# Conditioned FFN on one core: the beginning rebuilt (the q product, x's head sums, the order of the first loads)

## Chip, cores and metric

The kernel runs on one core of a Trainium2 chip. The metric is the device time of one execution in microseconds, the median of several runs; the profile is one further execution with the hardware profiler on.

## What is computed

x is 64 x 64 x 512 (batch, token, feature), cond is 64 x 256. Cut to what matters, the reference is:

```python
q_emb = relu(cond @ W3 + b3)                       # (64, 512)
x1 = (64 * x + x.sum(axis=1, keepdims=True)) * q_emb[:, None, :]
y = relu(x1 @ W2 + b2)                             # (64, 64, 512)
gates = top2(softmax(y @ W_router + b_router))     # six experts
out = x + y @ W_base + b_base + (y @ A_s) @ B_s + sum_e gates_e * (y @ A_r[e]) @ B_r[e]
```

## The kernel before

**Tiling.** The 4096 tokens are cut into 8 groups of 512 (eight batches of 64 tokens). The 512 features are four chunks of 128 partitions. For a group, m1 multiplies x1 with W2 (a bank of PSUM for each chunk of y), h gives router logits and the low-rank products, and m2 multiplies y with W_base into four tiles of 128 tokens. Each product of two f32 matrices is made of three matmuls: both operands are split into a rounded part "hi" (ScalarE copies it into the type fp32r) and a rest "lo" (VectorE or GpSimd subtract), and hi\*hi, lo\*hi and hi\*lo are added in PSUM.

**The first group** is prepared in another way than the rest. Its x comes in token order in four tiles of 128 tokens (L229) and TensorE transposes them, 16 transposes (L740), into four banks, one for each feature chunk. VectorE then works inside those banks: `sum_head` (L506 to L513) sums over the tokens of a batch and adds 64 x, `scale_head` (L515) multiplies by q, ScalarE makes x_hi out of the bank (`x1_split_head`, L375) and `rest_head` (L523) makes x_lo from the bank and x_hi. q itself is 16 matmuls with W3 as the weights, read with a stride of four columns, and cond (turned, 64 columns) as the moving side (`q`, L767); `q_relu` (L364) turns each of the four results into a chunk of qT. Dummy matmuls on a zero tile (`keep_warm`, L724) fill in.

**The later groups** are turned on VectorE (L474), summed (L479, L486), scaled by q on GpSimd (L308), split on ScalarE (`x1_split`, L344) and their rest is taken on VectorE out of SBUF (`x1_rest`, L491).

**What sets the order** is a hand-written program for each engine, with semaphores between them; there is no planner. On TensorE: dummies, the turns of cond, 16 turns of x, q's matmuls (L879 to L886), `m1_first` (L774 to L816), then h and m2 of group 0, then the other groups. On GpSimd: the rests of W2 in four pieces (L316 to L318), of the router and low-rank matrix Wd (L320), of W_base in four pieces (L321), then the scaling of group 1. SyncE issues the loads in the order x (4 tiles), W3 (2 halves), W2 (4), W_base and the small ones (L228 to L243). ScalarE issues cond, b2 and b3 (L336 to L338). cond and b2 are turned together and copied in one piece.

`m1_first` runs its 48 matmuls (4 chunks k of the features in, 4 tiles m out, 3 terms) in the order in which operands come to be, first k=0 and k=1 for all m, then k=2 and k=3 for the tiles 0 and 1, then for 2 and 3:

```python
for tiles in ((0, 1), (2, 3)):
    for k in range(KC // 2, KC):
        pe.wait_ge(x1_hi_ready, k + 1)
        pe.wait_ge(W2_lo_ready, k + 1)
        for m in tiles:
            chunk(m, k, W2_hi, x1_hi)
            chunk(m, k, W2_lo, x1_hi)
            pe.wait_ge(x1_lo_ready, k + 1)
            last = chunk(m, k, W2_hi, x1_lo)
```

Of the kernel before, what the change touches and what calls it, by code (L numbers as in the profile page):

```python
# [22 lines left out]
def adaln_ffn(nc, x, cond, W3, b3, W2, b2, W_base, b_base, A_s, B_s, A_r, B_r, W_router, b_router, out):  # L23
    F32 = mybir.dt.float32
# [24 lines left out]
    WARM_LOAD, WARM_W3, WARM_HALF, WARM_Q = 8, 1, 2, 1  # L49
# [7 lines left out]
    with ctx:  # L57
# [42 lines left out]
        vsum_head = sb("vsum_head", [P, KC, BG])  # L100
# [5 lines left out]
        cond_sb = sb("cond_sb", [B + KC, Q])  # L106
        condT = sb("condT", [P, KC + QC * B])
        qT = sb("qT", [P, KC, B])
        b3_sb = sb("b3_sb", [P, KC])
        b2_sb = condT[:, B:B + KC]  # L110
# [23 lines left out]
        m2_ps = [bank(f"m2_ps{t}") for t in range(TT)]  # L134
        m1_ps = [bank(f"m1_ps{m}") for m in range(KC - 1)] + [m2_ps[2]]
        hT = bank("hT")
        q_ps = m1_ps
        head_ps = [m2_ps[0], m2_ps[1], m2_ps[3], hT]
# [7 lines left out]
        cond_loaded, W3_loaded, b3_loaded = sem("cond_loaded"), [sem(f"W3_loaded{k}") for k in range(QC)], sem("b3_loaded")  # L146
        W2_loaded = [sem(f"W2_loaded{c}") for c in range(KC)]
# [66 lines left out]
        def _(sp):  # L214
# [12 lines left out]

            for t in range(TT):  # L228
                sp.dma_start(x_nat[0][:, t, :], x_groups[0][:, t, :]).then_inc(head_loaded[t], 16)  # L229
            for k in range(QC):  # L230
                sp.dma_start(W3_sb[:, k, :], W3[k * P:(k + 1) * P, :]).then_inc(W3_loaded[k], 16)
# [44 lines left out]
        def _(pool):  # L276
# [58 lines left out]
        def _(act):  # L335
            act.dma_start(cond_sb[0:B, :], cond).then_inc(cond_loaded, 16)  # L336
            act.dma_start(cond_sb[B:B + KC, 0:P], b2.rearrange("(k p) -> k p", p=P)).then_inc(cond_loaded, 16)
# [21 lines left out]
            nc.scalar.activation(condT[:, :], m1_ps[0][:, 0:KC + QC * B], ACT.Copy).then_inc(condT_copied, 1)  # L359
# [59 lines left out]
            def step(g, par):  # L419
# [8 lines left out]
                for m in range(KC):  # L428
                    relu(g, m, first)
                    if m == 0 and not first and not second:  # L430
                        hw_split(slice(0, TG), g)
# [35 lines left out]
        def _(dve):  # L467
# [255 lines left out]
        def _(pe):  # L723
# [13 lines left out]
            for t in range(TT):  # L737
                pe.wait_ge(head_loaded[t], 16)
                for c in range(KC):
                    turn = nc.tensor.transpose(head_ps[c][:, t * P:(t + 1) * P],  # L740
                                               x_nat[0][:, t, :].rearrange("p (f c) -> p c f", c=KC)[:, c], ident[:, :])
                    if t == TT - 1:
                        turn.then_inc(head_turned, 1)
# [212 lines left out]
```

## Time and profile before

| | |
|---|---|
| median of 3 runs | 236.16 us (236.14 to 236.66) |
| the profiled execution's own time | 236.26 us |
| its span, first to last instruction | 234.1 us |
| TensorE busy | 229.5 us, 98% of the span |
| VectorE, ScalarE, GpSimd busy | 165.8, 86.4 and 48.9 us |
| HBM read and written | 18.89 MB and 8.39 MB |

The own time is the span and 2.2 us around it. "PE" is TensorE's matmuls, "PEld" its weight loads, DVE is VectorE, ACT ScalarE, POOL GpSimd, SP SyncE. Busy matmul time counts the latency of each, so the pitch from one start to the next is what counts. PSUM tiles are grouped under one name: m_ps stands for the banks m1_ps and m2_ps.

### The profile page before, as it was taken

The numbers are of one execution on the slowest core, as the hardware profiler recorded it, in microseconds if no ns is written. First come the engines' busy times: TensorE is split into PE (matmuls) and PEld (weight loads), VectorE is DVE, ScalarE is ACT, GpSimd is POOL, SyncE is SP. The second block draws the span as 40 slices with busy tenths as digits, with TensorE's granted clock in tenths as the row PEclk, the third lists the DMA queues.
The fourth block names the chain that finished last, engine by engine and source line by source line (L and its number), as shares of the span: only waits on it lengthen the run. The fifth ranks groups of instructions, "written<-read, shape, count | busy, mean of one in ns | idle before, by whom it ended". The sixth has DMA issues, their size and how long they took to land.

```text
span 234.1 us, 3090 instructions
## 1 busy us (share of the span) xinstructions
PE 229.5 (98%) x1007; PEld 188.3 (80%) x1007; DVE 165.8 (71%) x309; ACT 86.4 (37%) x171; POOL 48.9 (21%) x57
## 2 busy tenths in 40 slices
PE   7999999999999999999999999999999999999994
PEld 3977888888888888888888888888888888888883
DVE  0685979899889966596939969399656966064344
ACT  3178632646036330535116240263306351252430
POOL 6089334032212211013012211022111030000000
PEclk9999999999999999999999999999999999999999
DMA  6999903509270723626053641709020360104004
GB/s 207 313 229 229 276 5 79 137 3 315 67 187 4 250 111 69 144 107 255 10 134 69 194 167 26 185 4 345 12 34 0 141 218 14 21 0 179 3 0 179
DMA packets 32505, 28.80 MB, mean 123 GB/s; under 512 B 5817, under 2 KB 22909, under 8 KB 32494
## 3 DMA queue, kind: packets, MB, share of 16 engines
q1 hardware_dynamic: 30682, 28.50, 43.1%
q10 hardware_dynamic: 1812, 0.17, 0.6%
q8 instruction: 6, 0.10, 0.2%
q14 instruction: 5, 0.04, 0.0%
HBM read 18.89 MB, written 8.39 MB: 117 GB/s over the span
## 4 chain that ended last, share of the span: by engine, by line
PE 97%; DVE 1%; ACT 1%; issue 0%; DVEq 0%
PE m_ps L750 78%; PE hT L750 9%; PE m_ps L777 5%; PE m_ps L727 2%; DVE out_nat L628 1%; PE m_ps L740 1%; PE m_ps L769 1%; PE hT L740 0%; ACT qT L367 0%; ACT W_hi L373 0%; ACT x_hi L378 0%; PE m_ps L734 0%; DVE idle L468 0%; PE hT L877 0%; PE m_ps L733 0%
## 5 line engine op out<-in xcount | busy, mean ns | idle before, releaser
L308 POOL TENSOR_TENSOR x_full<-x_sum,qT 128x512 f32<-128x512 f32 x28 | 32.2, 1150 | 134.6 <-DVE x_sum L486 134.6
L353 ACT ACTIVATE y_hi<-m_ps,condT 128x512 fp32r<-128x512 f32 x32 | 22.0, 687 | 77.5 <-PE m_ps L750 77.2
L750 PE MATMUL m_ps<-Wb_lo,y_hi 128*128 128x512 f32 x128 | 49.8, 389 | 0.0
L750 PE MATMUL m_ps<-Wb_hi,y_lo 128*128 128x512 f32 x128 | 49.8, 389 | 0.0
L750 PE MATMUL m_ps<-Wb_hi,y_hi 128*128 128x512 f32 x128 | 49.8, 389 | 0.0
L750 PE MATMUL m_ps<-x_hi,W_hi 128*128 128x512 f32 x112 | 43.6, 389 | 0.0
L750 PE MATMUL m_ps<-x_hi,W_lo 128*128 128x512 f32 x112 | 43.6, 389 | 0.0
L500 DVE TENSOR_TENSOR y_lo<-m_ps,y_hi 128x512 fp32r<-128x512 f32 x32 | 21.6, 674 | 30.4 <-ACT m_ps L355 30.4
L750 PE MATMUL m_ps<-x_lo,W_hi 128*128 128x512 f32 x112 | 41.8, 389 | 0.0
L474 DVE STREAM_TRANSPOSE xT<-x_quart 128x512 f32<-128x512 f32 x28 | 30.3, 1083 | 0.0
L750 PEld LDWEIGHTS m_ps<-Wb_hi,y_hi 128*128 128x128 f32 x128 | 24.0, 188 | 5.0
L750 PEld LDWEIGHTS m_ps<-Wb_hi,y_lo 128*128 128x128 f32 x128 | 24.0, 188 | 5.0
L750 PEld LDWEIGHTS m_ps<-Wb_lo,y_hi 128*128 128x128 f32 x128 | 24.0, 188 | 5.0
L347 ACT ACTIVATE x_hi<-x_full 128x512 fp32r<-128x512 f32 x28 | 17.6, 629 | 19.1 <-POOL x_full L308 19.0
L750 PEld LDWEIGHTS m_ps<-x_hi,W_hi 128*128 128x128 f32 x112 | 21.0, 188 | 4.4
L750 PEld LDWEIGHTS m_ps<-x_hi,W_lo 128*128 128x128 f32 x112 | 21.0, 188 | 4.4
L750 PEld LDWEIGHTS m_ps<-x_lo,W_hi 128*128 128x128 f32 x112 | 21.0, 188 | 4.3
L628 DVE TENSOR_TENSOR out_nat<-m_ps,x_nat 128x512 f32<-128x512 f32 x32 | 20.5, 680 | 2.1 <-PE m_ps L750 2.1
L355 ACT ACTIVATE m_ps<-m_ps,condT 128x512 f32<-128x512 f32 x32 | 21.0, 655 | 0.0
L486 DVE SCALAR_TENSOR_TENSOR x_sum<-xT,vsum 128x512 f32<-128x512 f32 x28 | 19.4, 693 | 2.1
L494 DVE TENSOR_TENSOR x_lo<-x_full,x_hi 128x512 fp32r<-128x512 f32 x28 | 19.1, 706 | 1.6 <-ACT x_hi L347 1.6
L479 DVE TENSOR_REDUCE vsum<-xT 128x8 f32<-128x512 f32 x28 | 19.0, 679 | 0.3
(99 smaller groups left out, 256.5 us busy)
## 6 DMA issues: line engine op xcount, KB each, us to landing
out_dram<-out_nat SPq DMA_DIRECT2D x32, 256.0 KB, 2.2
x_quart<-in_x_dram SPq DMA_DIRECT2D x28, 256.0 KB, 4.5
x_nat<-in_x_dram SPq DMA_DIRECT2D x7, 1024.0 KB, 6.1
gatesT<-wT SPq DMA_DIRECT2D x28, 48.0 KB
x_nat<-in_x_dram SPq DMA_DIRECT2D x4, 256.0 KB, 3.7
W_f<-in_L_cond_W_dram SPq DMA_DIRECT2D x4, 256.0 KB, 6.7
Wb_f<-in_L_ffn_W_base_dram SPq DMA_DIRECT2D x1, 1024.0 KB, 9.2
W_sb<-in_L_cond_W_dram SPq DMA_DIRECT2D x2, 256.0 KB, 5.0
```

Source lines behind the costliest of these rows:

```text
L308: nc.gpsimd.tensor_tensor(per_batch(x1_full[:, c, :]), per_batch(x1_sum[:, c, :]), qT[:, c, bass.ds(BG * g, BG)].unsqueeze(2).to_broadcast ...
L347: nc.scalar.activation(x1_hi[par][:, c, :], x1_full[:, c, :], ACT.Copy).then_inc(x1_hi_ready, 1)
L353: nc.scalar.activation(y_hi[:, m, :], m1_ps[m][:, :], ACT.Relu, bias=b2_sb[:, m:m + 1]).then_inc(y_hi_ready, 1)
L355: nc.scalar.activation(m1_ps[m][:, :], m1_ps[m][:, :], ACT.Relu, bias=b2_sb[:, m:m + 1]).then_inc(y_full_ready, 1)
L474: nc.vector.transpose(xT[c % 2][:, :], x_quart[par][:, :, :].rearrange("p b (i c) -> p c b i", c=KC)[:, c]).then_inc(xT_ready, 1)
L479: nc.vector.tensor_reduce(vsum[c % 2][:, :], per_batch(xT[c % 2][:, :]), AX.X, ALU.add).then_inc(vsum_ready, 1)
L486: nc.vector.scalar_tensor_tensor(out=per_batch(x1_sum[:, c, :]), in0=per_batch(xT[c % 2][:, :]), scalar=float(N), in1=vsum[c % 2][:, :].un ...
L494: nc.vector.tensor_tensor(x1_lo[par][:, c, :], x1_full[:, c, :], x1_hi[par][:, c, :].bitcast(F32), ALU.subtract).then_inc(x1_lo_ready, 1)
L500: nc.vector.tensor_tensor(y_lo[:, m, :], m1_ps[m][:, :], y_hi[:, m, :].bitcast(F32), ALU.subtract).then_inc(y_lo_ready, 1)
L628: nc.vector.tensor_tensor(out_nat[par][:, t, :], m2_ps[t][:, :], x_nat[par][:, t, :], ALU.add).then_inc(out_ready, 1)
L750: mm = nc.tensor.matmul(psum, lhsT, rhs, start=start and i == 0, stop=stop and i == len(terms) - 1)
L777: return nc.tensor.matmul(m1_ps[m][:, :], W[:, k, m * P:(m + 1) * P], x1[0][:, k, :], start=k == 0 and W is W2_hi and x1 is x1_hi, stop=k ...
```

## The change

Only the beginning is touched; the loop over the groups is the same.

- **q.** Only q's first chunk is still made directly (W3 strided as weights, two matmuls). The other three come from `q_others`: cond as weights (64 columns), W3 streamed contiguously, 256 columns for each matmul, four of them. The result lies with batches on the partitions; ScalarE copies it in two pieces to SBUF, TensorE turns it back in three transposes, then the three `q_relu`. These transposes stand inside `m1_first`.
- **x's sums by token halves.** The banks of the head hold two feature chunks for 256 tokens each, so that the first half can be summed when two tiles of x are there. The products with q go out of PSUM into SBUF: chunk 0 once into x1_hi directly and once into x1_full, the others into x1_full. ScalarE splits chunks 1 to 3 from there with `x1_split`, and the rests are taken with `x1_rest` out of SBUF, chunk 1's on GpSimd.
- **Loads.** W3's first (upper) half is issued ahead of the last tile of x.
- **The rest.** b2 is turned by itself after the first tile of x. Two single dummies stand behind the second and third tile of x, in place of one and two and one around q. `m1_first` takes the tiles in the order 0, 3, 2 and then 1. In the second half both x_hi terms of a pair of tiles go ahead of the wait for x_lo. The last piece of Wb_hi is made after the first relu. Group 1's first sum moves behind one more `y_rest`.

```diff
-    WARM_LOAD, WARM_W3, WARM_HALF, WARM_Q = 8, 1, 2, 1
+    WARM_LOAD, WARM_X = 8, 1
...
+        head_ps = [ctx.enter_context(nc.psum_tensor(f"head_ps{i}", [P, 2, 512], F32)) for i in range(2)]
+        q_rows = x1_sum[0:B, 0, 0:(KC - 1) * P]
...
             for t in range(TT):
+                if t == TT - 1:
+                    load_W3(0)
                 sp.dma_start(x_nat[0][:, t, :], x_groups[0][:, t, :]).then_inc(head_loaded[t], 16)
+            load_W3(1)
...
                 W_rest(W2_lo[:, c, :], W2_f[:, c, :], W2_hi[:, c, :], W2_lo_ready)
+                if c == 1:
+                    pool.wait_ge(x1_hi_ready, 2)
+                    pool.wait_ge(x1_lo_ready, 1)
+                    W_rest(x1_lo[0][:, 1, :], x1_full[:, 1, :], x1_hi[0][:, 1, :], x1_lo_ready)
...
             q_relu(0)
-            q_relu(1)
             W2_split(0)
-            q_relu(2)
-            x1_split_head(0)
-            q_relu(3)
-            x1_split_head(1)
+            for half in range(2):
+                act.wait_ge(q_rows_done, half + 1)
+                feats = slice(half * (P // 2), (half + 1) * (P // 2))
+                nc.scalar.activation(q_rows.rearrange("b (c f) -> b c f", f=P)[:, :, feats],
+                                     m1_ps[1 + half][0:B, 0:D // 2].rearrange("b (f c) -> b c f", c=KC)[:, 1:KC],
+                                     ACT.Copy).then_inc(q_rows_copied, 1)
             W2_split(1)
+            for c in range(1, KC):
+                q_relu(c)
+            x1_split(0, 0, 1)
             W2_split(2)
-            x1_split_head(2)
             W2_split(3)
+            x1_split(0, 0, 2)
+            x1_split(0, 0, 3)
...
+            sum_head(0, 0)
+            add_head(0, 0, 1)
+            sum_head(0, 1)
+            sum_head(1, 0)
+            add_head(1, 0, 3)
+            dve.wait_ge(qT_ready, 1)
+            dve.wait_ge(x1_sum_ready, 2)
+            nc.vector.tensor_tensor(by_half(x1_hi[0][:, 0, :]), head_chunk(0), q_spread(0),
+                                    ALU.mult).then_inc(x1_hi_ready, 1)
+            full_head(0)
+            dve.wait_ge(x1_full_ready, 1)
+            x1_rest(0, 0, 0)
+            full_head(1)
+            add_head(0, 1, 2)
+            sum_head(1, 1)
+            add_head(1, 1, 4)
+            full_head(2)
+            full_head(3)
+            dve.wait_ge(x1_lo_ready, 2)
+            x1_rest(0, 0, 2)
+            x1_rest(0, 0, 3)
...
+            turn_head(0)
+            pe.wait_ge(condT_copied, 1)
+            pe.wait_ge(b2_loaded, 16)
+            nc.tensor.transpose(m1_ps[0][:, QC * B:QC * B + KC], b2_rows[:, :], ident[0:KC, 0:KC]).then_inc(b2_turned, 1)
+            for t in range(1, TT - 1):
+                turn_head(t)
+                keep_warm(WARM_X)
...
+            def q_others(k, half):
+                cols = slice(half * (D // 2), (half + 1) * (D // 2))
+                mm = nc.tensor.matmul(m1_ps[1 + half][0:B, 0:D // 2], condT[:, cond_cols(k)], W3_sb[:, k, cols],
+                                      start=(k == 0), stop=(k == QC - 1))
...
                 pe.wait_ge(W2_hi_ready, 1)
-                for m in range(KC - 1):
-                    pe.wait_ge(qT_ready, m + 1)
-                    chunk(m, 0, W2_hi, x1_hi)
+                chunk(0, 0, W2_hi, x1_hi)
+                chunk(3, 0, W2_hi, x1_hi)
+                pe.wait_ge(q_rows_copied, 2)
+                chunk(2, 0, W2_hi, x1_hi)
+                for c in range(1, KC):
+                    last = nc.tensor.transpose(m1_ps[1][:, (c - 1) * B:c * B], q_rows[:, (c - 1) * P:c * P],
+                                               ident[0:B, 0:B])
+                last.then_inc(q_done, 1)
...
                         for m in tiles:
                             chunk(m, k, W2_hi, x1_hi)
                             chunk(m, k, W2_lo, x1_hi)
-                            pe.wait_ge(x1_lo_ready, k + 1)
+                        pe.wait_ge(x1_lo_ready, k + 1)
+                        for m in tiles:
                             last = chunk(m, k, W2_hi, x1_lo)
...
+            pe.wait_ge(b2_copied, 1)
+            q_first(0)
+            q_others(0, 0)
+            turn_head(TT - 1)
+            q_others(0, 1)
+            q_first(1)
+            for half in range(2):
+                q_others(1, half)
```

## Rows read from the trace of the kernel before

**Rows 1.** The page: TensorE's granted clock in 40 slices, in tenths.

```profile
PEclk9999999999999999999999999999999999999999
```

**Rows 2.** Chain that ended last, the beginning: start us, us, what.

```profile
12.47 11.47 PE m_ps L777 x48
...
28.70 22.44 PE m_ps L750 x99
```

**Rows 3.** Timeline, TensorE: start us, us, engine line op out<-in xcount [idle before].

```profile
1.27 3.59 PE L727 MATMUL m_ps<-idle 128*128 128x512 bf16 x8 [1.27 <-DVE idle L468]
...
4.97 0.37 PE L734 MATMUL m_ps<-ident,cond_sb 64*128 64x64 f32 x1
...
6.19 0.84 PE L740 MATMUL m_ps<-ident,x_nat 128*128 128x128 f32 x3
...
7.04 0.56 PE L740 MATMUL m_ps<-ident,x_nat 128*128 128x128 f32 x3
...
7.56 0.52 PE L740 MATMUL m_ps<-ident,x_nat 128*128 128x128 f32 x3
...
8.04 0.38 PE L727 MATMUL m_ps<-idle 128*128 128x512 bf16 x1
8.25 1.40 PE L769 MATMUL m_ps<-condT,W_sb 128*128 128x64 f32 x6
9.49 0.59 PE L727 MATMUL m_ps<-idle 128*128 128x512 bf16 x2
9.92 1.40 PE L769 MATMUL m_ps<-condT,W_sb 128*128 128x64 f32 x6
...
23.78 0.39 PE L750 MATMUL hT<-y_hi,Wd_hi 128*128 128x512 f32 x1
```

**Rows 4.** Timeline, VectorE, the head of group 0.

```profile
7.88 0.69 DVE L507 TENSOR_REDUCE vsum_head<-m_ps 128x8 f32<-128x512 f32 x1 [6.67 <-PE m_ps L740]
8.60 0.70 DVE L510 SCALAR_TENSOR_TENSOR m_ps<-m_ps,vsum_head 128x512 f32<-128x512 f32 x1
9.21 0.68 DVE L507 TENSOR_REDUCE vsum_head<-m_ps 128x8 f32<-128x512 f32 x1
...
13.77 0.70 DVE L510 SCALAR_TENSOR_TENSOR m_ps<-m_ps,vsum_head 128x512 f32<-128x512 f32 x1
14.58 0.70 DVE L519 TENSOR_TENSOR m_ps<-m_ps,qT 128x512 f32<-128x512 f32 x1
...
17.91 0.68 DVE L526 TENSOR_TENSOR x_lo<-m_ps,x_hi 128x512 fp32r<-128x512 f32 x1
```

**Rows 5.** Timeline, ScalarE, the same stretch.

```profile
10.49 0.72 ACT L367 ACTIVATE qT<-m_ps,b_sb 128x64 f32<-128x64 f32 x2 [4.84 <-PE m_ps L769]
11.11 0.62 ACT L373 ACTIVATE W_hi<-W_f 128x512 fp32r<-128x512 f32 x1
...
15.31 0.60 ACT L378 ACTIVATE x_hi<-m_ps 128x512 fp32r<-128x512 f32 x1 [1.12 <-DVE m_ps L519]
```

**Rows 6.** Timeline, GpSimd, the rests of the weights.

```profile
11.81 1.27 POOL L314 TENSOR_TENSOR W_lo<-W_f,W_hi 128x512 fp32r<-128x512 f32 x1 [7.02 <-ACT W_hi L373]
13.75 2.54 POOL L314 TENSOR_TENSOR W_lo<-W_f,W_hi 128x512 fp32r<-128x512 f32 x2 [0.67 <-ACT W_hi L373]
...
17.75 1.30 POOL L314 TENSOR_TENSOR Wd_lo<-Wd_f,Wd_hi 128x512 fp32r<-128x512 f32 x1
```

**Rows 7.** All instructions of L308 and of L494: duration ns min/median/max, starts.

```profile
L308 POOL TENSOR_TENSOR x_full<-x_sum,qT x28: 1043/1046/1422, 25.7 to 191.3; 128x512 f32<-128x512 f32 x28
...
L494 DVE TENSOR_TENSOR x_lo<-x_full,x_hi x28: 649/682/1531, 38.6 to 196.4; 128x512 fp32r<-128x512 f32 x28
```

**Rows 8.** Timelines of VectorE and of GpSimd where these two extremes lie.

```profile
39.20 1.53 DVE L494 TENSOR_TENSOR x_lo<-x_full,x_hi 128x512 fp32r<-128x512 f32 x1
...
38.76 1.42 POOL L308 TENSOR_TENSOR x_full<-x_sum,qT 128x512 f32<-128x512 f32 x1 [1.41 <-DVE x_sum L486]
```

**Rows 9.** Time to landing of W3's halves (issued at 2.67 and 3.14).

```profile
DMA to landing us min/median/max: 4.8/5.0/5.1
```

More of the change, by code:

```diff
@@ L128, in adaln_ffn @@
         pick_one = sb("pick_one", [S, P])
-        m2_ps = [bank(f"m2_ps{t}") for t in range(TT)]
+        head_ps = [ctx.enter_context(nc.psum_tensor(f"head_ps{i}", [P, 2, 512], F32)) for i in range(2)]
+        m2_ps = [head_ps[0][:, 0, :], head_ps[0][:, 1, :], bank("m2_ps2"), head_ps[1][:, 0, :]]
         m1_ps = [bank(f"m1_ps{m}") for m in range(KC - 1)] + [m2_ps[2]]
-        hT = bank("hT")
-        q_ps = m1_ps
-        head_ps = [m2_ps[0], m2_ps[1], m2_ps[3], hT]
+        hT = head_ps[1][:, 1, :]
         x_loaded = [sem(f"x_loaded{i}") for i in range(2)]
@@ L429, in step @@
                     relu(g, m, first)
+                    if first and m == 0:
+                        Wb_split(KC - 1)
                     if m == 0 and not first and not second:
@@ L510, in sum_head, with add_head @@
+            def add_head(h, pr, summed):
+                dve.wait_ge(vsum_head_ready, summed)
                 nc.vector.scalar_tensor_tensor(
[L511 to L512 removed]
+                    out=head_half(pr, h), in0=head_half(pr, h), scalar=float(N),
+                    in1=vsum_head[:, h, pr, :].unsqueeze(2).to_broadcast([P, BG, N]),
@@ L731, in _, with turn_head @@
             pe.wait_ge(ident_ready, 1)
-            pe.wait_ge(cond_loaded, 32)
-            nc.tensor.transpose(m1_ps[0][:, 0:B + KC], cond_sb[:, 0:P], ident[0:B + KC, 0:B + KC])
-            last = nc.tensor.transpose(m1_ps[0][:, cond_cols(1)], cond_sb[0:B, P:2 * P], ident[0:B, 0:B])
+            pe.wait_ge(cond_loaded, 16)
+            for k in range(QC):
+                last = nc.tensor.transpose(m1_ps[0][:, cond_cols(k)], cond_sb[:, k * P:(k + 1) * P], ident[0:B, 0:B])
             last.then_inc(condT_done, 1)
-            for t in range(TT):
+            def turn_head(t):
                 pe.wait_ge(head_loaded[t], 16)
                 for c in range(KC):
-                    turn = nc.tensor.transpose(head_ps[c][:, t * P:(t + 1) * P],
+                    begin = (c % 2) * (TG // 2) + (t % 2) * P
+                    turn = nc.tensor.transpose(head_ps[c // 2][:, t // 2, begin:begin + P],
                                                x_nat[0][:, t, :].rearrange("p (f c) -> p c f", c=KC)[:, c], ident[:, :])
-                    if t == TT - 1:
+                    if t % 2 == 1 and c % 2 == 1:
                         turn.then_inc(head_turned, 1)
-            keep_warm(WARM_W3)
+            turn_head(0)
[5 more added lines that the diff above has]
+                keep_warm(WARM_X)
             def product(psum, terms, start, stop):
@@ L782, in m1_first @@
                 pe.wait_ge(W2_hi_ready, 1)
-                for m in range(KC - 1):
-                    pe.wait_ge(qT_ready, m + 1)
-                    chunk(m, 0, W2_hi, x1_hi)
+                chunk(0, 0, W2_hi, x1_hi)
[6 more added lines that the diff above has]
+                last.then_inc(q_done, 1)
                 pe.wait_ge(W2_lo_ready, 1)
-                for m in range(KC - 1):
+                for m in (0, 2, 3):
                     chunk(m, 0, W2_lo, x1_hi)
+                pe.wait_ge(x1_lo_ready, 1)
+                for m in (0, 2, 3):
+                    chunk(m, 0, W2_hi, x1_lo)
                 pe.wait_ge(qT_ready, KC)
-                chunk(KC - 1, 0, W2_hi, x1_hi)
-                chunk(KC - 1, 0, W2_lo, x1_hi)
-                pe.wait_ge(x1_lo_ready, 1)
-                for m in range(KC):
-                    chunk(m, 0, W2_hi, x1_lo)
+                chunk(1, 0, W2_hi, x1_hi)
+                chunk(1, 0, W2_lo, x1_hi)
+                chunk(1, 0, W2_hi, x1_lo)
                 for k in range(1, KC // 2):
```

101 lines of the change are left out of this document (44 added, 57 removed).

## The prediction

> **What bounds the kernel now.** I read the chain that ended last first. Behind 12.47 us it is TensorE alone: 48 matmuls of `m1_first` in 11.47 us, then 99 in 22.44, a pitch of 0.227 us [rows 2]. Nothing after the beginning waits, so the change can move only two things: when `m1_first` starts, and how much it loses inside. Its own work is 48 x 0.227 = 10.88 us; h begins at 23.78 [rows 3], 11.31 after the start, so 0.43 is lost inside. **The mark to beat is 23.78.** Then the timelines of the first 24 us: TensorE turns x until 8.04 and does q until past 11.2 [rows 3]; VectorE begins at 7.88, when the last tile is turned [rows 4]; ScalarE waits 4.84 us for q and makes qT at 10.49 [rows 5]. The start is a meeting of q and x's sums.
>
> **The clock.** The granted clock reads full in all slices [rows 1], but eight dummies of 512 columns take 3.59 us, 0.43 apiece as at 1.2 GHz; four transposes take 0.85 from 6.19 and 0.48 from 7.56 [rows 3]. The level of 2.4 GHz comes at about 7.1. Up to 6.2 the new order issues the same work, so I keep 7.1.
>
> **The change, part by part.**
>
> *Up to W3.* The last tile's four transposes leave this place (-0.48), b2's own turn comes in (one more small transpose, at most 0.37 [rows 3]; I take 0.3), and there is one dummy more (0.21). The first W3 matmul stays at 8.25 [rows 3]. Chunk 1 of tile 1 is then turned near 6.9 and VectorE starts its first half sum at about 7.2, not 7.88.
>
> *The loads.* W3's first half lands 4.8 us after its issue at 2.67, at 7.5 [rows 9], and is used at 8.25: nobody waits. A place earlier it gains nothing, and the last x tile, then at about 7.5, is wanted at 8.9. This part is worth 0; its cover is 0.7 us on either side.
>
> *q.* 16 matmuls of 64 columns cost 0.21 each (six in 1.24) and three dummies go. In come two of those and four `q_others` of 256 columns with an f32 moving side, which no row shows. Lower bound: the 512-column pitch by columns, 0.11. Upper: the 64-column one times four, 0.83. They are far apart; I take the middle, 0.48, as a weight load of the old form costs something that does not grow with columns. TensorE: 8.25 first chunk, 8.45 `q_others`, 8.93 to 9.41 the last x tile (its chunk 1 at 9.05), 9.41 `q_others`, 9.89 the first chunk's second half, then two `q_others` to 11.06.
> The Trainium skill (FP8 and Floating Point Precision, TensorE Precision Notes) says that true FP32 takes four passes; 256 columns at 2.4 GHz would be 0.43, and no run here shows it yet. By it every time below would be some 0.1 earlier.
>
> *The start.* x: 9.05 + 0.32 (from the transpose at 7.56 to the sum at 7.88) = 9.37 for the second half's sum, +0.72 the addition [rows 4], +0.81 the product (13.77 to 14.58) = 10.90. q: 9.89 + 0.57 (9.92 to 10.49) + 0.35 = 10.81. VectorE is the later by a hair. The product goes straight to x1_hi; the next engine follows 0.73 later (14.58 to 15.31 [rows 4, 5]): **`m1_first` starts at 11.63, 0.84 earlier.** W2_hi is there at 11.4.
>
> *Inside.* ScalarE copies q's rows by 12.0 (W2_split 0.62 between, two copies of some 0.3). TensorE does chunks 0 and 3, then 2, then three transposes: 0.5 that the old order did not have, and back to work at 12.9. qT's second chunk: 12.7 + 0.35 ScalarE + 0.35 = VectorE's product of chunk 1 at s = 13.40. Nine more matmuls for k=0 end at 14.95, k=1 at 17.67. x1_hi of chunk 1: s + 0.73 + 0.63 = 14.76, in time. VectorE's next steps are two of 0.61, one of 0.72, one of 0.81, so chunk 2's product is at s + 2.75 and its x1_hi at s + 4.14 = 17.54, in time by 0.13.
>
> *The new wait.* Before, `rest_head` read the bank and one SBUF tile, and ran 0.68 beside GpSimd (17.91, inside 17.75 to 19.05 [rows 4, 6]). `x1_rest` reads two SBUF tiles. That form has a median of 682 ns and a maximum of 1531 [rows 7], and that maximum stands against GpSimd's maximum: VectorE's at 39.20 ends at 40.73, 0.55 after GpSimd's at 40.18, which itself took 1.42 for 1.05 because the rest before it held on until 39.28 [rows 7, 8]. They take turns, whole instructions at a time. In the head GpSimd has no pause: chunk 1's rest from s + 1.44, then pieces of W2_lo at a pitch of 1.25 (two in 2.54 [rows 6]), the last from s + 3.94 to s + 5.23 = 18.63. VectorE asks for chunk 2's rest at s + 4.14, 0.2 too late: done at 18.63 + 0.55 = 19.18; TensorE wanted it at 17.67 + 4 x 0.227 = 18.58. Then Wd_lo, queued behind W2_lo, has its turn (1.29 less 0.14 for what it did while it waited, as 1.05 became 0.90 above) to 20.33, and chunk 3's rest ends at 20.88. TensorE wanted it at 19.18 + 6 x 0.227 = 20.54. 14 matmuls remain: end at 20.88 + 3.17 = **24.05, against 23.78: +0.27.**
> The Trainium skill says the same (SBUF — State Buffer, Who interferes with whom): a VectorE instruction with two SBUF inputs contends with a GpSimd instruction that reads SBUF, by an exclusive lock held for the whole instruction, and issue order decides who blocks. By this rule, the trace agrees (1531 ns). It speaks against this change; without it the sum would be 0.6 faster than before.
>
> *Behind it.* y's splits follow the last products by ScalarE; Wb_hi's last piece inside costs relu 1 a step of 0.6, and GpSimd reaches Wb_lo's first piece at some 22, before m2 asks at 25. The regrouping of terms makes m1_done of tile 0 two matmuls later, 0.45, hidden by h starting only 3 us on. I cost these at 0; if that cover is gone, y_lo's last chunk is late next, by 0.1 to 0.3.
>
> **Sum.** 236.26 (own time) + 0.27 = 236.5; the own time lies 0.10 above the median, so **236.4 us.** With the start's bounds: at 0.11 a `q_others` s falls only to 13.1, as VectorE and ScalarE bind: 236.1; at 0.83, see below.
>
> **Rivals.**
> A, the forecast: start won, given back by the shared turns. 0.42.
> B, VectorE gets the first turn. Its request is only 0.2 behind GpSimd's start, and these are sums of five steps. Then chunk 2's rest is in time, W2_lo's last piece ends at 19.38 for 19.03, and m1 ends at 23.46: -0.32, 235.8. For it: the small gap. Against: every step from s on has its own row and s cancels. 0.18.
> C, no stall: TensorE runs through from 12.9, m1 ends at 17.67 + 24 x 0.227 = 23.11, -0.67, 235.5; with cheap `q_others` down to 235.3. For it: 27 of 28 rests of this form are near 0.68 [rows 7]. Against: only in the head is GpSimd busy without pause. 0.25.
> D, the other side: streaming W3 in f32 costs in proportion, 0.83. Then q's first chunk is at 10.59, the start at 12.2 and s at 14.4, one us later, with m1's end at 25.05: +1.27, 237.4. It decides from about 0.6 a matmul: above that q, not x, is the last to arrive, three `q_others` weigh on s, and the time is over 236.9. For it: nothing in the trace has an f32 moving side of this width. 0.13.
> E, the beginning only shifts its waits and nothing changes, 236.2. 0.02.
>
> **How the numbers follow.** A measurement of this kernel tells some 0.3%, 0.71 us, from no change: faster is below 235.45, slower above 236.87. A gives same 0.33, slower 0.09 (q's price above the middle); B same 0.15, faster 0.03; C faster 0.17, same 0.08; D slower 0.13; E same 0.02. In all faster 0.20, same 0.58, slower 0.22. Range 235.3 to 237.1: it takes in A to C with the bounds of q's price, and leaves most of D and C's edge out. A's own range is 236.1 to 236.9.
>
> **What would show it.** In the new profile: `m1_first`'s first matmul at 11.4 to 11.8; `q_others` at a pitch near 0.5; the turns of b2 and the three transposes 0.2 to 0.5 us of TensorE each; a rest (L494's successor) of over 1 us against W2_lo's last piece, and another against Wd_lo; TensorE waiting 0.6 and 0.3 us for them; h's first matmul near 24.05 and from there the old pitch. Wrong if the rests take 0.68 beside GpSimd (then C), if TensorE waits ahead of 12 us for x1_hi longer than before (D), if the 2.4 GHz level comes after 8 us, or if anything behind 24 us waits.

## The result and the profile after

The changed kernel takes 236.50 us (median of 22 runs, 236.09 to 238.54), the one before 236.03 (22 runs, 235.23 to 236.66), run in turns on the same chips. The ratio is 1.0039, with a 95% interval of 1.0024 to 1.0053: slower by some 0.4%. The profiled execution took 236.53 us against 236.26, its span is 234.8 us against 234.1. The forecast was 236.4, with 235.3 to 237.1 as its range; 18 of the 22 runs lie between 236.09 and 236.92, four at 238.3 to 238.5.

The timeline of TensorE in the changed kernel, from the first matmul with W3 to h (a line stands for consecutive instructions of one form; several lines between are left out):

```profile
7.60 0.47 PE L820 MATMUL m_ps<-condT,W_sb 128*128 128x64 f32 x2
8.00 0.65 PE L828 MATMUL m_ps<-W_sb,condT 128*64 128x256 f32 x2
8.57 0.75 PE L784 MATMUL head_ps<-ident,x_nat 128*128 128x128 f32 x4
9.25 0.65 PE L828 MATMUL m_ps<-W_sb,condT 128*64 128x256 f32 x2
9.83 0.68 PE L820 MATMUL m_ps<-condT,W_sb 128*128 128x64 f32 x2
10.44 1.08 PE L828 MATMUL m_ps<-W_sb,condT 128*64 128x256 f32 x4
11.64 0.97 PE L836 MATMUL m_ps<-x_hi,W_hi 128*128 128x512 f32 x3
12.53 0.40 PE L847 MATMUL m_ps<-ident,x_sum 64*128 64x64 f32 x3
...
18.44 0.39 PE L836 MATMUL m_ps<-x_hi,W_lo 128*128 128x512 f32 x1
19.16 0.74 PE L836 MATMUL m_ps<-x_lo,W_hi 128*128 128x512 f32 x2 [0.34 <-DVE x_lo L527]
...
20.43 0.39 PE L836 MATMUL m_ps<-x_hi,W_lo 128*128 128x512 f32 x1
20.87 0.73 PE L836 MATMUL m_ps<-x_lo,W_hi 128*128 128x512 f32 x2
...
24.18 0.39 PE L800 MATMUL head_ps<-y_hi,Wd_hi 128*128 128x512 f32 x1
```

`m1_first` begins at 11.64, 0.83 us earlier than before, but h at 24.18, 0.40 later than the 23.78 of [rows 3]: from start to h it is 12.54 us against 11.31. Two steps between matmuls stand out against the pitch of 0.227: 0.73 to 19.16 and 0.44 to 20.87. Behind each the next step is again long (two matmuls end 0.74 and 0.73 after the start of the first, where 0.61 is usual). What they waited for stands in VectorE's and GpSimd's timelines, the answer to [rows 7, 8]:

```profile
12.21 1.08 DVE L527 TENSOR_TENSOR x_lo<-x_full,x_hi 128x512 fp32r<-128x512 f32 x1
...
17.50 1.61 DVE L527 TENSOR_TENSOR x_lo<-x_full,x_hi 128x512 fp32r<-128x512 f32 x1 [0.17 <-ACT x_hi L372]
19.03 1.78 DVE L527 TENSOR_TENSOR x_lo<-x_full,x_hi 128x512 fp32r<-128x512 f32 x1
...
16.02 2.54 POOL L335 TENSOR_TENSOR W_lo<-W_f,W_hi 128x512 fp32r<-128x512 f32 x2
18.60 1.67 POOL L335 TENSOR_TENSOR Wd_lo<-Wd_f,Wd_hi 128x512 fp32r<-128x512 f32 x1
20.22 3.00 POOL L335 TENSOR_TENSOR Wb_lo<-Wb_f,Wb_hi 128x512 fp32r<-128x512 f32 x2
```

Read the ends: GpSimd's W2_lo ends at 18.56, VectorE's rest at 19.11; GpSimd's Wd_lo at 20.27, VectorE's second rest at 20.81. Each time 0.55 us of work follow the other's end, and Wd_lo itself became 1.67 us long where it takes 1.30 [rows 6], because it had to let the rest end first. Chunk 0's rest at 12.21 was held too: it took 1.08 us and ended 0.54 after GpSimd's first piece of W2_lo (12.75). That one cost nothing that shows: the next product waits for qT's second chunk, which is ready at the same moment, 13.29.

Behind h a second loss shows, near 55 us, in group 1. TensorE's last matmul starts at 231.15 against 230.52, 0.63 later. Of that 0.40 are from the head and 0.23 come behind h, 0.18 of them in the two long steps here (0.31 to 55.31 and 0.34 to 55.65; before, 0.23 and 0.24):

```profile
55.00 0.39 PE L800 MATMUL head_ps<-y_hi,Wd_lo 128*128 128x512 f32 x1
55.31 0.50 PE L800 MATMUL head_ps<-y_lo,Wd_hi 128*128 128x512 f32 x1
55.65 0.40 PE L800 MATMUL head_ps<-Wb_hi,y_hi 128*128 128x512 f32 x1
```

VectorE is late with y_lo. Its chain goes back without a pause of note to the routing of group 0, where one subtraction on 24 columns, read from two SBUF tiles, met GpSimd's Wu_lo:

```profile
31.24 1.00 DVE L592 TENSOR_TENSOR logit<-h_nat,lmax 128x24 f32<-128x24 f32 x1
...
30.90 1.30 POOL L335 TENSOR_TENSOR Wu_lo<-Wu_f,Wu_hi 128x512 fp32r<-128x512 f32 x1
```

Before, it met it as well, but took 0.66 us:

```profile
30.84 0.66 DVE L551 TENSOR_TENSOR logit<-h_nat,lmax 128x24 f32<-128x24 f32 x1
...
30.16 1.29 POOL L314 TENSOR_TENSOR Wu_lo<-Wu_f,Wu_hi 128x512 fp32r<-128x512 f32 x1
```

GpSimd's Wu_lo now comes 0.74 us later (30.90 against 30.16) and VectorE's step only 0.40, so it stands longer.

### The profile page after: what moved, and what is told of

It is laid out like the page before. It is cut to its first block, busy times and chain, and to the rows that moved or that the text cites. A ratio compares the mean times of both kernels' runs of the same rounds, so it can differ in the third digit from the quotient of the medians.

```text
span 234.8 us, 3094 instructions
## 1 busy us (share of the span) xinstructions
PE 229.7 (98%) x1005; PEld 186.1 (79%) x1005; DVE 168.4 (72%) x309; ACT 86.9 (37%) x173; POOL 51.4 (22%) x58
## 4 chain that ended last, share of the span: by engine, by line
PE 93%; DVE 4%; ACT 1%; issue 0%; DVEq 0%
PE m_ps L800 44%; PE head_ps L800 44%; PE m_ps L836 2%; PE m_ps L769 2%; DVE x_lo L527 1%; DVE out_nat L669 1%; PE head_ps L784 1%; DVE x_full L558 1%; DVE head_ps L545 1%; PE m_ps L828 0%; PE m_ps L820 0%; DVE x_hi L568 0%; ACT qT L396 0%; ACT x_hi L372 0%; DVE vsum_head L540 0%
## 5 line engine op out<-in xcount | busy, mean ns | idle before, releaser
L378 ACT ACTIVATE y_hi<-m_ps,b_sb 128x512 fp32r<-128x512 f32 x32 | 22.1, 689 | 78.0 <-PE m_ps L800 76.6
L800 PE MATMUL head_ps<-Wb_hi,y_hi 128*128 128x512 f32 x96 | 37.4, 389 | 0.0
L800 PE MATMUL head_ps<-Wb_hi,y_lo 128*128 128x512 f32 x96 | 37.4, 389 | 0.0
L800 PE MATMUL head_ps<-Wb_lo,y_hi 128*128 128x512 f32 x96 | 37.3, 389 | 0.0
L527 DVE TENSOR_TENSOR x_lo<-x_full,x_hi 128x512 fp32r<-128x512 f32 x31 | 23.6, 783 | 1.8 <-ACT x_hi L372 1.8
L380 ACT ACTIVATE m_ps<-m_ps,b_sb 128x512 f32<-128x512 f32 x32 | 21.0, 658 | 0.0
L800 PEld LDWEIGHTS head_ps<-Wb_hi,y_lo 128*128 128x128 f32 x96 | 18.0, 188 | 3.8
L800 PEld LDWEIGHTS head_ps<-Wb_lo,y_hi 128*128 128x128 f32 x96 | 18.0, 188 | 3.7
L800 PEld LDWEIGHTS head_ps<-Wb_hi,y_hi 128*128 128x128 f32 x96 | 18.0, 188 | 3.7
L478 ACT ACTIVATE h_head<-head_ps,h_bias 32x128 f32<-32x128 f32 x32 | 11.5, 360 | 12.8 <-PE head_ps L800 12.2
```

Source lines behind the costliest of these rows:

```text
L378: nc.scalar.activation(y_hi[:, m, :], m1_ps[m][:, :], ACT.Relu, bias=b2_sb[:, m:m + 1]).then_inc(y_hi_ready, 1)
L380: nc.scalar.activation(m1_ps[m][:, :], m1_ps[m][:, :], ACT.Relu, bias=b2_sb[:, m:m + 1]).then_inc(y_full_ready, 1)
L478: nc.scalar.activation(h_head[q * S:(q + 1) * S, :], hT[0:S, q * P:(q + 1) * P], ACT.Identity, bias=h_bias[0:S, 0:1]).then_inc(h_head_read ...
L527: nc.vector.tensor_tensor(x1_lo[par][:, c, :], x1_full[:, c, :], x1_hi[par][:, c, :].bitcast(F32), ALU.subtract).then_inc(x1_lo_ready, 1)
L800: mm = nc.tensor.matmul(psum, lhsT, rhs, start=start and i == 0, stop=stop and i == len(terms) - 1)
```

## The experiments

Each ran in turns with the kernel before, whose median was 235.72 to 235.93 us in those turns. So the ratio in the last column compares two rows better than their medians do. The high level of TensorE's clock comes at another time in each profiled execution (last section), which moves the start by more than 2 us. The stretch from `m1_first`'s first matmul to h's does not follow it: e1, e5, e10 and e11 have 11.56 to 11.58 us with starts from 11.16 to 13.80, the changed kernel, e4 and e6 12.54 with starts from 11.64 to 12.02.

| kernel | start, h, between (us) | median, runs | ratio to before, 95% |
|---|---|---|---|
| before | 12.47, 23.78, 11.31 | 236.03, 22 | 1 |
| changed | 11.64, 24.18, 12.54 | 236.50, 22 | 1.0024 to 1.0053 |
| e1 rests from PSUM | 13.47, 25.05, 11.58 | 235.64, 12 | 0.9982 to 1.0000 |
| e2 GpSimd holds back | 12.06, 24.26, 12.20 | 236.25, 11 | 1.0012 to 1.0046 |
| e3 old, rests from SBUF | 12.70, 25.51, 12.81 | 237.37, 4 | 1.0045 to 1.0074 |
| e4 Wu's rest earlier | 11.92, 24.46, 12.54 | 236.38, 12 | 1.0008 to 1.0053 |
| e5 is e1 and e4 | 11.16, 22.73, 11.57 | 235.33, 12 | 0.9969 to 1.0003 |
| e6 load order back | 12.02, 24.56, 12.54 | 237.69, 6 | 1.0062 to 1.0113 |
| e7 q all direct | 11.98, 24.58, 12.60 | 236.78, 10 | 1.0023 to 1.0063 |
| e8 is e7, e1 and e4 | 12.07, 24.42, 12.35 | 236.77, 12 | 1.0013 to 1.0063 |
| e9 is e8 with dummies | 12.32, 23.71, 11.39 | 235.48, 12 | 0.9988 to 1.0005 |
| e10 is e5, chunk 0 sooner | 11.41, 22.97, 11.56 | 235.23, 12 | 0.9970 to 1.0016 |
| e11 is e10, more dummies | 13.80, 25.36, 11.56 | 235.49, 13 | 0.9971 to 0.9996 |

### e1: the rests read from PSUM

```diff
-                nc.vector.tensor_tensor(by_half(x1_full[:, c, :]), head_chunk(c), q_spread(c),
+                out = x1_full[:, c, :] if c < 2 else head_ps[0][:, c - 2, :]
+                nc.vector.tensor_tensor(by_half(out), head_chunk(c), q_spread(c),
...
-            x1_rest(0, 0, 2)
-            x1_rest(0, 0, 3)
+            for c in (2, 3):
+                dve.wait_ge(x1_hi_ready, c + 1)
+                nc.vector.tensor_tensor(x1_lo[0][:, c, :], head_ps[0][:, c - 2, :],
+                                        x1_hi[0][:, c, :].bitcast(F32), ALU.subtract).then_inc(x1_lo_ready, 1)
```

(ScalarE's two splits read the same banks.)

> The changed kernel, but the products of chunks 2 and 3 go into the two PSUM banks that chunks 0 and 1 have left, and ScalarE and VectorE read them there, so that a rest has one SBUF input. Theory (VectorE and GpSimd take turns for the second SBUF input): both rests fall from 1.61 and 1.78 us to about 0.68, TensorE's two waits at 18.4 and 20.4 us go, h's first matmul comes at 23.2 to 23.4 instead of 24.18, and the time is 0.8 to 0.9 us lower, 235.6. Rival (the rests are late because x1_hi of chunk 2 is late, whoever holds a port): the rests may get shorter, but TensorE still waits 0.3 us or more at each, h comes at 23.8 or later and the time is within 0.4 us of 236.5.

Measured: 235.64 us, 0.86 below the changed kernel (1.1 by the ratios). Both rests run beside GpSimd, which is never idle there (VectorE's timeline, then GpSimd's):

```profile
19.31 1.29 DVE L584 TENSOR_TENSOR x_lo<-head_ps,x_hi 128x512 fp32r<-128x512 f32 x2
...
17.84 2.54 POOL L335 TENSOR_TENSOR W_lo<-W_f,W_hi 128x512 fp32r<-128x512 f32 x2
20.40 1.29 POOL L335 TENSOR_TENSOR Wd_lo<-Wd_f,Wd_hi 128x512 fp32r<-128x512 f32 x1
```

Two rests in 1.29 us, and from start to h it is 11.58, so 0.96 less. h came at 25.05 and not at 23.3, since in this execution (237.37 us) the clock's high level came more than 4 us later; the stretch and the median carry the verdict. The rival falls: x1_hi comes at the same distance from the start (the first of the two rests begins 5.84 us behind it here, 5.86 in the changed kernel), and TensorE has no step above 0.25 us between 16 and 56 us.

### e2: GpSimd holds back

```diff
             pool.wait_ge(Wd_hi_ready, 1)
+            pool.wait_ge(x1_lo_ready, KC)
```

> The changed kernel, but GpSimd waits for all four rests before Wd_lo. Theory (turns): the first rest stays at 1.6 us (W2_lo's last piece holds it), the second falls from 1.78 to about 0.7, so TensorE's second wait, 0.2 us and a slow restart, goes; h at 23.85 instead of 24.18, time lower by 0.3 us, 236.2. Wd_lo and Wb_lo end a good 0.6 us later, which nobody should feel. Rival (the second rest is long for another reason, for example that it waits for ScalarE): it stays at 1.7 us, and nothing changes, 236.5.

```profile
17.93 1.61 DVE L528 TENSOR_TENSOR x_lo<-x_full,x_hi 128x512 fp32r<-128x512 f32 x1 [0.17 <-ACT x_hi L373]
...
19.46 0.68 DVE L528 TENSOR_TENSOR x_lo<-x_full,x_hi 128x512 fp32r<-128x512 f32 x1
```

The first rest, held by W2_lo's last piece, stays at 1.61 us; the second falls from 1.78 to 0.68 as nothing else was changed than what GpSimd does at that moment. The stretch loses 0.34 us. The median is 0.25 lower, but the two intervals overlap, so here the trace carries the verdict; h came at 24.26 and not at 23.85, since the start was 0.42 later. So each of the two turns has its own share: 0.34 for Wd_lo's, the rest of e1's 0.96 for that of W2_lo.

### e3: the same rests in the old kernel

```diff
-                nc.vector.tensor_tensor(per_batch(head_ps[c][:, :]), per_batch(head_ps[c][:, :]),
+                nc.vector.tensor_tensor(per_batch(x1_full[:, c, :]), per_batch(head_ps[c][:, :]),
```

(and the splits and rests read x1_full.)

> The kernel before, with one thing of the change alone: the head's products go to SBUF and the splits and rests are read from there. Theory (turns): GpSimd makes W2_lo, Wd_lo and Wb_lo from 11.8 us on nearly without pause, so the four rests become 1.1 to 1.8 us each against 0.68, VectorE's head falls behind by 2 us or more, TensorE waits, and h comes 0.8 to 1.6 us later than 23.78: 236.9 to 237.7. Rival (reading from SBUF costs nothing, as this form has a median of 682 ns): h at 23.8, time within 0.2 us of 236.1.

```profile
15.88 1.19 DVE L526 TENSOR_TENSOR x_lo<-x_full,x_hi 128x512 fp32r<-128x512 f32 x1
...
19.12 1.78 DVE L526 TENSOR_TENSOR x_lo<-x_full,x_hi 128x512 fp32r<-128x512 f32 x2
...
20.35 0.50 PE L777 MATMUL m_ps<-x_lo,W_hi 128*128 128x512 f32 x1 [1.47 <-DVE x_lo L526]
```

This one part of the change alone makes the old kernel 0.6% slower (237.37 us), with one wait of 1.47 us and 1.50 us more from start to h. Three of the four rests took 1.16 to 1.19 us and the last 0.68, less than I expected for each. How long one takes depends on how far GpSimd is in its own instruction when the rest is asked for: the three end 0.55 us after GpSimd's (13.84, 17.07 and 20.30 against 13.29, 16.52 and 19.75), and the last falls into a pause of GpSimd's. VectorE is later each time, and the delays add up.

### e4: Wu's rest ahead of one scaling

```diff
             scale(1, 0)
-            scale(1, 1)
             pool.wait_ge(Wu_hi_ready, 1)
             W_rest(Wu_lo[:, :], Wu_f[:, :], Wu_hi[:, :], Wu_lo_ready)
+            scale(1, 1)
```

> The changed kernel, but GpSimd makes the rest of Wu before the scaling of group 1's second chunk, not after. Theory for the 0.2 us that TensorE loses near 55 us: the small subtraction of the logits at 31.24 us took 1.00 us (0.66 before) because it has two SBUF inputs and GpSimd was in Wu_lo; VectorE's chain stays 0.7 us behind and y_lo comes late. Then here the subtraction takes 0.2 to 0.3 us, the wait near 55 us goes, h's first matmul stays at 24.18 and the time is lower by 0.2 us, 236.3. Rival (that wait comes from the shift by 0.4 us of the whole start): it stays, and the time is 236.5.

```profile
31.52 0.18 DVE L592 TENSOR_TENSOR logit<-h_nat,lmax 128x24 f32<-128x24 f32 x1
...
55.31 0.40 PE L800 MATMUL head_ps<-y_hi,Wd_lo 128*128 128x512 f32 x1
55.55 0.40 PE L800 MATMUL head_ps<-y_lo,Wd_hi 128*128 128x512 f32 x1
55.78 0.39 PE L800 MATMUL head_ps<-Wb_hi,y_hi 128*128 128x512 f32 x1
```

The subtraction takes 0.18 us (1.00), with GpSimd idle beside it, and the two long steps near 55 us are gone (0.24 and 0.23), though the stretch to h is still 12.54. In the trace the cause of these two steps is settled. In the medians it is 0.12 us, less than these runs can tell.

### e5: both cures

> Both cures together: the rests of chunks 2 and 3 read from PSUM, and Wu's rest made before the scaling of group 1's second chunk. Theory: the two losses lie in different places (19 to 21 us and 55 us), so they add: 0.9 and 0.2 us less than the changed kernel, 235.4; no pause of TensorE over 0.3 us between 12 us and the end except the restarts in the first three microseconds of m1_first. Rival (a third wait takes the place): a new pause of VectorE's or ScalarE's making appears behind 24 us and the time is that of the first cure alone, 235.6 to 235.7, or more.

235.33 us, 1.17 below the changed kernel (1.25 by the ratios), where 0.9 and 0.2 were expected. Behind 13 us no step between TensorE's matmuls exceeds 0.25 us. No third wait took their place.

### e6: the old order of the loads

```diff
-                if t == TT - 1:
-                    load_W3(0)
                 sp.dma_start(x_nat[0][:, t, :], x_groups[0][:, t, :]).then_inc(head_loaded[t], 16)
+            load_W3(0)
             load_W3(1)
```

> The changed kernel with SyncE's loads in the old order: W3's first half behind the last tile of x. Theory: nobody waits for either in the new order (W3's half landed at 7.16 and is used at 7.6, the last x tile landed at 7.90 and is used at 8.57), and in the old order W3's half would land near 7.5 to 7.9: no change, 236.4 to 236.6. Rival (the order is what lets q start early): the first W3 matmul slips by 0.2 to 0.5 us, the last to arrive is q, so m1_first and the time slip by as much, 236.7 to 237.0.

```profile
7.06 0.38 PE L768 MATMUL m_ps<-idle 128*128 128x512 bf16 x1
7.80 0.65 PE L819 MATMUL m_ps<-condT,W_sb 128*128 128x64 f32 x2 [0.36 <-DMA W_sb<-in_L_cond_W_dram]
```

My theory fell, the rival held in its direction: TensorE waits 0.36 us for W3, the start is at 12.02, and the time is higher (237.69 in 6 runs that spread from 236.86 to 238.61; the profiled one, 236.86, is the fastest, 0.33 above that of the changed kernel, and its start 0.38). The stretch from start to h is the same, 12.54. By the ratios the old order costs 1.2 us; the trace explains 0.4 of it, and the rest stays open: the slower runs were not profiled.

### e7, e8 and e9: q direct, and what the clock makes of it

```diff
-            q_first(0)
-            q_others(0, 0)
-            turn_head(TT - 1)
-            q_others(0, 1)
-            q_first(1)
-            for half in range(2):
-                q_others(1, half)
+            for c in range(KC):
+                q_direct(0, c)
+            turn_head(TT - 1)
+            for c in range(KC):
+                q_direct(1, c)
```

(`q_direct` is the old `q`; the copies of rows and the three transposes go, and TensorE waits behind the first matmul of `m1_first` for all four chunks of qT.)

> The changed kernel with q made as before (W3 as strided weights, 64 columns of cond, for all four chunks), the rest of the change as it is; no copies of rows and no three transposes. Theory: a direct matmul costs 0.47 us (two records at 0.233), a streamed one 0.58, so q's first chunk is finished 0.3 us later behind four directs than behind one direct and one streamed, m1_first starts at about 11.9 to 12.0, q's last chunk is ready near 12.7, and what the transposes cost (0.65 us) is saved but waited for; the two rests still lose their turns, so h comes within 0.3 us of 24.2 to 24.5 and the time is 236.5 to 236.8. Rival (the transposes inside m1_first are a real loss): h at 23.6 or earlier and 235.9.

> q all direct, with both cures (rests from PSUM, Wu's rest earlier). Theory: without the turns the end of m1_first is set by TensorE's own work and by when x1_hi comes; q direct starts 0.3 us later and saves transposes it then waits for, so 235.4 to 235.8, no better than the streamed form with both cures. Rival (streaming W3 is a loss once the turns are cured): 235.1 or lower.

e7 took 236.78 us, e8 236.77. For e7 that is the number expected; e8 missed by 1 us. Both have something that neither theory knew. TensorE in three stretches of e7 (us, busy and count, granted clock, DMA share, GB/s):

```profile
10.00:12.00 2.00, 1.72 (x9) 0.99 1.11 375
12.50:15.20 2.70, 2.70 (x8) 0.50 1.18 209
15.50:20.00 4.50, 4.50 (x21) 1.00 1.06 222
```

The first two of them in e8:

```profile
10.00:12.00 2.00, 1.84 (x8) 0.87 1.12 366
12.50:15.20 2.70, 2.70 (x8) 0.56 1.10 198
```

With q all direct the granted clock falls to its lower level, 1.2 GHz, around the start of `m1_first`, and stays there for some 3 us: 8 matmuls in 2.7 us, 0.427 apart. In the changed kernel and the one before it is 1.00 in this stretch.

Every run lists its mean granted clock, and this tells the price of the fall. In e8 three runs of 12 have 1.000 and took 235.38 to 235.58 us, which is what my theory said; the other nine have 0.991 to 0.993 and took 236.54 us or more. In e7 nine runs of 10 have 0.985 to 0.993, and the one with 1.000 took 236.64, in their midst. So in e8 the fall costs some 1.3 us (median of the nine against the three), and in e7 nothing that shows. There the two rests still run against GpSimd (1.59 and 1.78 us), yet TensorE has no step above 0.25 us between 16 and 56 us: slowed by the clock, it comes when they are done. So the fall likely takes the place of the waits and does not add to them. e7's number was right with a fall in it that the theory did not have.

e9 is e8 with the old kernel's dummies around q:

```diff
-            for c in range(KC):
-                q_direct(0, c)
+            for c in range(KC - 1):
+                q_direct(0, c)
+            keep_warm(2)
             turn_head(TT - 1)
```

(one more dummy behind the second half, the fourth chunk last.)

> The kernel of e8 (q all direct, rests from PSUM, Wu's rest earlier) with the three dummy matmuls of the old kernel put back around q: two behind the first half of the first three chunks, one behind the second half, the fourth chunk last. In e8 the granted clock fell to 0.56 between 12.5 and 15.2 us and TensorE's pitch was 0.427 us there. Theory (64-column matmuls alone leave TensorE too lightly used, and the dummies or the 256-column streams keep the clock up): the granted clock stays at 1.00 from 10 to 20 us, no pitch of 0.427 behind 12 us, the start is 0.2 to 0.4 us later than e8's 12.07, and the time falls from 236.8 to 235.6 to 236.0. Rival (the fall has to do with the pause ahead of m1_first, or with chance): the clock falls as in e8 and the time is 236.8 or more.

The same two stretches in e9:

```profile
10.00:12.00 2.00, 2.00 (x12) 1.00 1.09 377
12.50:15.20 2.70, 2.58 (x12) 1.00 1.23 247
```

The clock stays at 1.00, the time falls by 1.29 us to 235.48 (1.0 by the ratios), and the 12 runs lie within 0.41 us. All 12 have a mean granted clock of 1.000, against 3 of 12 in e8 and 1 of 10 in e7, so it is not chance. In e7 and e8 TensorE had done eight direct matmuls and four transposes between 7.4 and 11.8 us, then paused 0.2 to 0.3 us for x1_hi; in e9 it had three dummies among them and no such pause before 12.3. The pause is not what lets the clock fall in e8, as it falls while the last direct matmul is still running, which ends at 11.84 (in e7 it falls at 11.97, at the end of the pause):

```profile
11.40:11.50 0.10, 0.10 (x2) 0.92 1.13 385
11.50:11.60 0.10, 0.10 (x2) 0.50 1.20 424
```

So the dummies hold the clock by what TensorE does ahead of the pause. Which of the three is needed, no run here shows.

### e10 and e11

```diff
             turn_head(TT - 1)
-            q_others(0, 1)
             q_first(1)
+            q_others(0, 1)
```

> The kernel of e5 with q's first chunk finished ahead of the second streamed matmul and not behind it. In the changed kernel VectorE had been ready for 0.35 us when qT's first chunk came, so q, not x, sets the start. Theory: q_relu comes 0.5 us earlier, the additions of x then set the start, so m1_first starts 0.3 us earlier than at e5's 11.16 (at the same clock), but the rows' copies and the three transposes come no earlier, so that at most 0.1 to 0.3 us of it is kept: 235.1 to 235.3 against 235.33. Rival (W3's second half is not there yet, it landed between 8.15 and 8.66): TensorE waits and nothing is gained, 235.3 to 235.6.

235.23 us against 235.33, within what these runs can tell; the start did not come earlier in the profiled one (11.41, with W3's first matmul 0.36 later; from that matmul to the start it is 3.98 us against 4.09). Not shown either way.

```diff
-    WARM_LOAD, WARM_X = 8, 1
+    WARM_LOAD, WARM_X = 8, 2
```

> The kernel of e10 with two dummies instead of one behind the second and the third tile of x (0.43 us more of TensorE before W3 at the high clock). In e5 and e10 four of 24 runs lay 1.6 to 2.3 us above the rest, in the kernel with direct q and dummies none of 12. Theory (the fuller use of TensorE in the first 9 us brings the high level in time in every run): the start moves from 11.4 to 11.5 to 11.8, the median rises by 0.1 to 0.4 us, to 235.3 to 235.6, and no run lies more than 1 us above the lowest. Rival (when the level comes is up to chance, whatever TensorE does): one to three of the dozen runs still lie 1.5 us or more above the lowest.

The rival held: one of 13 runs, the profiled one, took 237.47 us, the others 234.99 to 235.89. (One of 13 against four of 24 doesn't tell whether such runs became rarer.) Its transposes and dummies kept the long pitch (0.213 and 0.427 us) until about 10 us:

```profile
7.38 1.06 PE L773 MATMUL m_ps<-idle 128*128 128x512 bf16 x2
8.23 1.06 PE L788 MATMUL head_ps<-ident,x_nat 128*128 128x128 f32 x4
9.08 1.06 PE L773 MATMUL m_ps<-idle 128*128 128x512 bf16 x2
9.94 0.52 PE L824 MATMUL m_ps<-condT,W_sb 128*128 128x64 f32 x2
```

e1's did the same, with one dummy in each place:

```profile
7.38 0.63 PE L773 MATMUL m_ps<-idle 128*128 128x512 bf16 x1
7.81 1.06 PE L788 MATMUL head_ps<-ident,x_nat 128*128 128x128 f32 x4
8.66 0.63 PE L773 MATMUL m_ps<-idle 128*128 128x512 bf16 x1
9.09 0.53 PE L824 MATMUL m_ps<-condT,W_sb 128*128 128x64 f32 x2
```

(Here a dummy takes 0.43 us from start to start; the changed kernel's two between 6 and 8 us took 0.22.)

## Why the prediction was right, point by point

**The new wait** was the step that carried the forecast, and it stands to a tenth: s = 13.31 (13.40 forecast), the first rest done at 19.11 (19.18), the second at 20.81 (20.88), TensorE's waits 0.50 and 0.22 us (0.60 and 0.34). e1 and e2 show the cause by taking it away from VectorE's side and from GpSimd's; e3 puts it into the old kernel. The rule of the Trainium skill (SBUF — State Buffer, Who interferes with whom), that a VectorE instruction with two SBUF inputs contends with a GpSimd instruction that reads SBUF, agrees with all three (0.68 to 0.69 us a rest in e1, 0.68 for the freed one in e2, 1.16 to 1.19 for three of e3's). In [rows 7] only one of 28 rests had shown it. That chunk 0's rest would be held as well, 1.08 us, the forecast did not have; it cost nothing.

**h** came at 24.18, not 24.05. The missing term is the restart: the first step between matmuls behind a wait was 0.34 us and not 0.227. It happened twice, but only the second adds up, 0.11: the first is over before TensorE comes to its second wait, whose end VectorE sets.

**The start** came at 11.64, forecast 11.63, but by two errors that cancel. The clock's high level came at about 5.6 and not 7.1, so that W3's first matmul stood at 7.60, not 8.25. And q cost more, 2.23 us from there to the first chunk's second half (9.83) where I had 1.64. I read the 16 records of L769 as 16 matmuls, and the description of the kernel before counts 16 too; there are 8, two records each, 0.47 us a matmul. A streamed one, also two records, took 0.57 to 0.58 us (8.00 to 8.57), not 0.48, as its halves take 0.27 and 0.31 of which some is the change of weights. The last x tile's four transposes between them took 0.68 and not 0.48. So the first chunk was ready at 10.54 + 0.32 on ScalarE, and VectorE waited 0.35 us for it: q was the later, not x. The estimate from the four-pass figure of the Trainium skill (FP8 and Floating Point Precision, TensorE Precision Notes) was 0.43. The trace agrees where the weights don't change: the two records of the fourth streamed matmul (10.92 and 11.13) are 0.215 us apart, 0.43 for the matmul.

So the gain at the start is luck of the clock as far as its size goes. In the executions with the changed order the start follows the rise of the clock:

| | high level from | start |
|---|---|---|
| e5 | 4.1 | 11.16 |
| changed | 5.6 | 11.64 |
| e4 | 6.2 | 11.92 |
| e2 | 6.4 | 12.06 |
| e1 | 10.2 | 13.47 |

Between the last two, a rise at 7.1, as I had assumed it, would give a start near 12.4 (an estimate from these rows), hardly earlier than 12.47. The old order gains nothing from an early rise: in e3 it came at 4.1, TensorE then stood for a tile of x (0.90 us between two transposes at 5.88) and came to W3 at 8.27, as before. The forecast's sign of being wrong, a rise behind 8 us, came true in e1 and e11.

**The loads** I priced at 0, with 0.7 us of cover. e6 shows at least 0.4 us: with an earlier clock TensorE is at W3 at 7.1 to 7.6, and the cover that I had counted from 8.25 is gone. This step failed.

**Behind it** I priced at 0 as well. The trace shows 0.23 us behind h, 0.18 of it near 55 us, by the same mechanism as in the head, two SBUF inputs beside GpSimd, on an instruction of 24 columns. The row was there before, 0.66 us for a subtraction, and the forecast left it out. This step failed too.

**The sum.** +0.27 was forecast. TensorE's last matmul is 0.63 later in the trace, the own time 0.27, the median of 22 runs 0.47. That the own time meets the forecast exactly is chance: the span grew by 0.63 us, but the time around it fell from 2.1 to 1.8 us, and so it did in every run of the changed order (1.75 to 1.78 in the medians, 1.9 to 2.0 with the old order, e3 among them). The forecast did not have this, and its reason stays open. The median before was 236.16 in 3 runs and is 236.03 in 22, so the forecast time is closer than the forecast change: +0.27 forecast, +0.47 measured.

**The rivals.** B (VectorE gets the first turn) and C (no stall) did not happen in the profiled executions of the changed kernel, e2 and e4: each had VectorE's request 0.2 us behind GpSimd's start, since both follow s. D (the price of streaming) was half right: dearer than forecast, but only by 0.1, and q was the last to arrive, as D had it. Outside the range lie the four runs at 238.3 to 238.5, for which no rival had a price.

**What the whole change is worth, part by part.** In the two profiled executions: start earlier by 0.83 us, most of it the clock's; turns of the two rests, -0.96 by e1; what is left inside `m1_first`, -0.27 (11.58 in e1 against 11.31 before), for which the three transposes and the longer steps around them are the likely cause, though no run takes them out alone; behind h, -0.23, nearly all of it the routing's subtraction. Cured of the second and the last it is e5, 235.33 us, 0.5 us under the kernel before in the same turns, with an interval (0.9969 to 1.0003) that still touches 1; e11, the same with two small additions, has 0.9971 to 0.9996. The old way of making q with its dummies, and all the rest of the change (e9), takes 235.48; the runs don't tell it from e5. None of its 12 runs lies 1.5 us above its median, but with 15 such runs of 116 in the other kernels of the new order (e6 left out) that can be chance. So streaming W3 is not needed for the time.

## What to carry to other kernels

Before an operand moves from PSUM to SBUF, count the SBUF inputs of the VectorE instruction that reads it, and see what GpSimd does at that moment: in these traces one input cost nothing beside it (0.68 us a rest), two made a rest 1.08 to 1.78 us long whenever GpSimd was at work, and a tile of 24 columns 1.00 us instead of 0.18. A maximum far from the median in a group of equal instructions is worth a look at what the other engine did. And look at the granted clock behind a stretch of small matmuls before you take dummies out of it: without the three, e8 lost 1.3 us in nine of 12 runs. An early part that looks faster in one profile may have had an earlier clock: compare stretches that begin behind the rise, or several executions.

## What the runs showed of the hardware that was not expected

- The high level of TensorE's clock came in the profiled executions at about 4.1 us (e3, e5), 4.3 to 5.2 (e10, e6, e8, e7), 5.6 (changed), 6.2 to 6.4 (e2, e4, e9), 7.1 (before) and 10.2 to 10.4 (e1, e11), each time with the same eight dummies as TensorE's first work; the granted clock of the profile reads 1.00 from the start all the same, and only the pitch shows the rise (a dummy 0.43 us from start to start, then 0.22). Where it came near 10 the execution took 237.4 to 237.5 us, 1.7 to 2.0 above the median of its kernel. Of the 22 runs of the changed kernel 4 lay at 238.3 to 238.5. That those had a late clock is likely, but their rise is not known. More dummies (e11) did not end it. The kernel before had no run of that kind in 118; why a late rise costs the old order less is not shown.
- A later fall of the clock does show in the granted clock (0.50 and 0.56 between 12.5 and 15.2 us in e7 and e8). It cost 1.3 us in e8, between its own runs with and without it, and nothing that shows in e7, where it likely took the place of the waits for the rests.
- Each f32 matmul of q stands in the trace as two records, 0.233 us each for 64 columns and 128 columns of weights; a transpose of an f32 tile is one.
- A VectorE instruction held by GpSimd ended 0.54 to 0.55 us after GpSimd's each time, six times in the heads of the changed kernel and e3, and the same instruction alone takes 0.68.
